# Third feed-forward of an eight-part kernel: weights rounded during the attention before it, maxima and rounding by pieces

## The reference, cut to what matters

```python
x = x + _L2_xattn_ref(_layernorm(x), ctx, ctx, w_q, w_k, w_v, w_o)       # fifth: 16 heads of 64
x = x + _L2_ffn_ref(_layernorm(x), clip_x, clip_down, w_gate, w_up, w_down)  # sixth

def _act_fake_quant(x, clip):            # one scale for the whole tensor
    scale = sigmoid(clip) * max(|x|) / 127
    return clamp(round(x / scale), -128, 127) * scale
def _weight_fake_quant(w):               # one scale for each row
    scale = max(|w|, axis=1) / 127
    return clamp(round(w / scale), -128, 127) * scale
def _L2_ffn_ref(x, clip_x, clip_down, w_gate, w_up, w_down):   # 352 inner units
    xq = _act_fake_quant(x, clip_x)
    h = _act_fake_quant(silu(xq @ Wq(w_gate).T) * (xq @ Wq(w_up).T), clip_down)
    return h @ Wq(w_down).T
```

## Time and profile before

| | us |
|---|---|
| median of three runs | 2153.54 (2153.01 to 2155.19) |
| the profiled execution's own time | 2155.52 |
| its span (what the profile covers) | 2153.7 |
| PE busy | 1917.7 (89%) |
| DVE busy | 1305.2 (61%) |
| ACT busy | 1291.8 (60%) |
| stage `ln2a` starts / `pair_layer` starts | 781.1 / 788.6 |
| `ln2f` starts / `ffn2_stage` starts / `ln3a` starts | 1629.1 / 1636.5 / 1673.7 |

### The profile page before, as it was taken

The page is one execution under the profiler, slowest core; times in us unless marked ns, Lnnn a source line. Parts: engine busy times, 40 slices in busy tenths (PEclk is TensorE's granted clock), DMA queues, the critical chain, the costliest instruction groups (busy, mean ns, idle before and its releaser), DMA issues. The chain is left out here.

```text
span 2153.7 us, 43741 instructions
## 1 busy us (share of the span) xinstructions
PE 1917.7 (89%) x17168; PEld 1360.0 (63%) x17168; DVE 1305.2 (61%) x3216; ACT 1291.8 (60%) x2074; POOL 130.7 (6%) x344
## 2 busy tenths in 40 slices
PE   6999999967768559999999999999994699999997
PEld 4677777734634546777777777777772456666663
DVE  6888888876545335554555545555445776666663
ACT  4999999954248115555555555555553356666664
POOL 4000000000022110000000000000000400000000
PEclk9999999977869669999999999999996789999998
DMA  6211111102070520000000000000000621111110
GB/s 230 57 46 44 44 46 45 38 16 70 8 183 2 153 78 1 1 2 1 1 1 1 2 1 1 2 1 2 1 1 11 199 57 47 42 47 46 46 37 17
DMA packets 55291, 87.71 MB, mean 41 GB/s; under 512 B 9865, under 2 KB 31421, under 8 KB 55089
## 3 DMA queue, kind: packets, MB, share of 16 engines
q1 hardware_dynamic: 54577, 83.87, 13.2%
q0 software_dynamic: 512, 1.05, 0.2%
HBM read 66.93 MB, written 17.96 MB: 39 GB/s over the span
## 5 line engine op out<-in xcount | busy, mean ns | idle before, releaser
L2315 ACT ACTIVATE a_prT<-bank 128x512 f32<-128x512 f32 (+1 forms) x448 | 232.7, 565 | 328.0 <-PE bank L2224 327.8
L1110 DVE CUSTOM_DVE_ANT_0 a_attn_junk<-wide,a_mask 128x801 f32<-128x801 f32 (+1 forms) x256 | 247.4, 991 | 123.2 <-PE wide L942 123.0
L1053 ACT ACTIVATE a_attn_prT<-bank 128x512 f32<-128x512 f32 (+1 forms) x448 | 237.0, 566 | 123.0 <-PE bank L959 110.5
L2340 DVE CUSTOM_DVE_ANT_0 a_sc<-wide,a_zeros 128x1024 f32<-128x1024 f32 (+1 forms) x256 | 243.1, 987 | 91.9 <-PE wide L2210 91.9
L1401 DVE CUSTOM_DVE_ANT_0 a_attn_sc<-wide,a_mask 128x801 f32<-128x801 f32 (+1 forms) x256 | 252.8, 988 | 12.0 <-PE wide L1252 10.2
L1268 PE MATMUL bank<-ident,a_attn_sc 128*128 128x128 f32 x1664 | 244.6, 275 | 15.2 <-ACT a_attn_prT L1360 14.1
L1268 PEld LDWEIGHTS bank<-ident,a_attn_sc 128*128 128x128 f32 x1664 | 198.8, 141 | 62.2 <-issue 42.3
L2224 PE MATMUL bank<-ident,a_sc 128*128 128x128 f32 x1664 | 231.3, 277 | 1.5 <-ACT a_prT L2315 1.5
L2224 PEld LDWEIGHTS bank<-ident,a_sc 128*128 128x128 f32 x1664 | 185.4, 141 | 54.4 <-issue 28.1
L2210 PE MATMUL wide<-a_kT,a_qT 64*128 64x512 f32 (+1 forms) x1024 | 211.0, 529 | 0.0
L2276 PEld LDWEIGHTS bank<-a_prT,a_vt 128*64 128x64 f32 x3328 | 180.3, 137 | 48.4 <-issue 47.0
(11 more groups left out here) (448 smaller groups left out, 2537.5 us busy)
## 6 DMA issues: line engine op xcount, KB each, us to landing
a_ks<-a_k_parts SPq DMA_DIRECT2D x384, 75.0 KB
a_k_parts<-a_proj_kp SPq DMA_DIRECT2D x24, 416.0 KB, 4.3
a_qx<-a_q_stack SPq DMA_DIRECT2D x384, 12.0 KB
moe_w1b<-in_e_w SPq DMA_DIRECT2D x15, 256.0 KB, 2.8
ctxT<-in_ctxT SPq DMA_DIRECT2D x4, 832.0 KB, 10.6
a_ctxn<-in_ctxn SPq DMA_DIRECT2D x4, 832.0 KB
m_q_stack<-m_proj_qp SPq DMA_DIRECT2D x9, 256.0 KB, 8.9
m_ks<-m_k_parts SPq DMA_DIRECT2D x24, 96.0 KB
```

Of the source, the lines that this page charges most:

```text
L1053: act.activation(prT[0:keys, u % PRT, kt:kt + m, :], bank_of(s, f"W{g}")[0:keys, 0:m * S].rearrange("p (t q) -> p t q", q=S), ACT.Exp).the ...
L1110: dve.tensor_tensor_reduce(junk[:, n % 2, 0:w], S_WIDE[n % 2][:, 0:w], mask(qt, at, w), 1.0, LOWEST, ALU.add, ALU.max, mx[:, p % 2, qt, e, ...
L2315: copy = lambda out, src: act.activation(out, src, ACT.Copy)
L2340: dve.tensor_tensor_reduce(sc[:, s % 2, h, at:at + w], S_WIDE[h][:, 0:w], zeros[:, 0:w], 1.0, LOWEST, ALU.add, ALU.max, mx[:, s % 2, h, p: ...
```

## The change

The weights of the sixth block are loaded by `ln2a` instead of `ln2f`, live in SBUF through the attention, and are rounded inside `pair_layer`, on VectorE at the end of steps 44 to 49 (a few instructions in each); ScalarE makes the exponential of the clip factors in step 44. In `ffn2_stage` the spreading of a maximum is one matmul with the column, broadcast along its free axis, as weights and the identity as moving operand, after which every partition takes the maximum of its own copy. `x` is rounded by halves, and the last step (subtracting the constant and writing bfloat16) is ScalarE's. The pieces run through three bank pairs instead of two, all chunks of the first half ahead of the second; VectorE takes each piece's maximum one piece later, and the six maxima are reduced at the end. `h` is rounded by pieces: two VectorE operations and one of ScalarE. The down projection has the tokens' `h` stationary, 24 matmuls of 128 columns, and its output comes untransposed; the scale of `w_down`'s rows is spread once over the partitions (`down_row`), and two VectorE operations for each of four groups of two tiles scale and add.

```diff
--- before.py
+++ after.py
@@ -627,158 +627,154 @@
...
-def ffn2_stage(core, w_gu, w_down, clips):
+def ffn2_stage(core, w, sig):
...
+        g_bank, u_bank, d_bank = core.bank[0:3], core.bank[3:6], core.bank[0:4]
+        tb, tb2 = core.bank[6][:, :].bitcast(BF16), core.bank[7][:, :].bitcast(BF16)
+        row_bank, top_bank = core.bank[5][:, 0:P], (core.bank[4][:, 0:P], core.bank[6][:, 0:P])
+        work = [(c, i) for c in range(2) for i in range(NC)]
...
         @block.tensor
...
+            pe.matmul(row_bank, am[:, 2 * NC:].broadcast_to([P, P]), core.ident[:, :], start=True, stop=True).then_inc(row_made, 1)
+            pe.wait_ge(col_ready, 1)
+            pe.matmul(top_bank[0], col[:, 0:1].broadcast_to([P, P]), core.ident[:, :], start=True, stop=True).then_inc(spread, 1)
+            pe.wait_ge(w_copied, 2)
+            pe.wait_ge(row_in, 1)
+            for n, (c, i) in enumerate(work):
+                if i == 0:
+                    pe.wait_ge(xq_ready, c + 1)
+                if n >= 3:
+                    pe.wait_ge(gu_read, n - 2)
+                rhs = xq[:, c * 512:(c + 1) * 512]
+                pe.matmul(g_bank[n % 3][0:pad(i), :], wgu[:, i, 0:pad(i)], rhs, start=True, stop=True)
+                pe.matmul(u_bank[n % 3][0:pad(i), :], wgu[:, NC + i, 0:pad(i)], rhs, start=True, stop=True).then_inc(gu_ready, 1)
+            pe.wait_ge(col_ready, 2)
+            pe.matmul(top_bank[1], col[:, 1:2].broadcast_to([P, P]), core.ident[:, :], start=True, stop=True).then_inc(spread, 1)
...
+                pe.wait_ge(hq_ready, NC * (c + 1))
...
+                    for i in range(NC):
+                        at = c * 512 + t * P
+                        ins = pe.matmul(d_bank[2 * c + t // 2][:, t % 2 * P:(t % 2 + 1) * P], hq[0:pad(i), i, at:at + P], wd[0:pad(i), i, :],
+                                        start=(i == 0), stop=(i == NC - 1))
+                    if t % 2 == 1:
+                        ins.then_inc(down_ready, 1)
...
         @block.scalar
...
+            act.activation(gs[0:1, 0, 0:1], core.ones[0:1, 0:1], ACT.Silu).then_inc(warm, 1)
...
+            act.wait_ge(row_made, 1)
+            act.activation(down_row[:, :], row_bank, ACT.Copy).then_inc(row_in, 1)
+            act.wait_ge(warm, 1)
+            for c in range(2):
+                cols = slice(c * 512, (c + 1) * 512)
+                act.wait_ge(rounded, c + 1)
+                act.activation(xq[:, cols], xr[:, cols], ACT.Identity, bias=back[:, :]).then_inc(xq_ready, 1)
+            act.wait_ge(scales, 1)
...
+                if n >= 3:
+                    act.wait_ge(gu_read, n - 2)
+                act.activation(gs[0:pad(i), n % 3, :], g_bank[n % 3][0:pad(i), :], ACT.Silu,
...
+            for n, (c, i) in enumerate(work):
+                cols = slice(c * 512, (c + 1) * 512)
+                act.wait_ge(h_rounded, n + 1)
+                act.activation(hq[0:pad(i), i, cols], h[0:pad(i), i, cols], ACT.Identity,
+                               bias=back[0:pad(i), :]).then_inc(hq_ready, 1)
...
         @block.vector
...
+            dve.memset(back[:, :], -ROUND)
+            dve.memset(part[:, :], 0.0)
+
+            def scale_of(r):
+                dve.wait_ge(spread, r + 1)
+                link(dve.tensor_reduce(top[:, r:r + 1], top_bank[r], X, ALU.max))
+                link(dve.tensor_scalar(sx[:, r:r + 1], top[:, r:r + 1], sig[:, r:r + 1], 1.0 / 127.0, ALU.mult, ALU.mult))
...
+            def magnitude(n):
+                c, i = work[n]
+                dve.wait_ge(gu_read, n + 1)
+                return dve.tensor_reduce(part[0:pad(i), n:n + 1], h[0:pad(i), i, c * 512:(c + 1) * 512], X, ALU.max,
+                                         apply_absolute_value=True)
+
+            dve.tensor_reduce(col[:, 0:1], core.xnT[:, :], X, ALU.max, apply_absolute_value=True).then_inc(col_ready, 1)
+            scale_of(0)
+            for c in range(2):
+                cols = slice(c * 512, (c + 1) * 512)
+                link(dve.tensor_scalar(xr[:, cols], core.xnT[:, cols], rx[:, 0:1], ROUND, ALU.mult, ALU.add))
+                dve.tensor_scalar(xr[:, cols], xr[:, cols], ROUND + 127.0, ROUND - 128.0, ALU.min, ALU.max).then_inc(rounded, 1)
+                if c == 0:
+                    dve.tensor_scalar(fs[:, :], am[:, 0:2 * NC], sx[:, 0:1], None, ALU.mult).then_inc(scales, 1)
+            dve.wait_ge(scales, 1)
...
+                dve.scalar_tensor_tensor(h[0:pad(i), i, c * 512:(c + 1) * 512], u_bank[n % 3][0:pad(i), :],
+                                         fs[0:pad(i), NC + i:NC + i + 1], gs[0:pad(i), n % 3, :],
...
+                if n > 0:
+                    magnitude(n - 1)
+            link(magnitude(2 * NC - 1))
+            dve.tensor_reduce(col[:, 1:2], part[:, :], X, ALU.max).then_inc(col_ready, 1)
+            scale_of(1)
+            for n, (c, i) in enumerate(work):
+                piece = h[0:pad(i), i, c * 512:(c + 1) * 512]
+                link(dve.tensor_scalar(piece, piece, rx[0:pad(i), 1:2], ROUND, ALU.mult, ALU.add))
+                dve.tensor_scalar(piece, piece, ROUND + 127.0, ROUND - 128.0, ALU.min, ALU.max).then_inc(h_rounded, 1)
+            dve.wait_ge(row_in, 1)
+            for g in range(4):
+                tiles = core.x[:, 2 * g:2 * g + 2, :]
+                dve.wait_ge(down_ready, g + 1)
+                dve.scalar_tensor_tensor(term[:, g, :, :], d_bank[g][:, 0:2 * D].rearrange("p (t d) -> p t d", d=D),
+                                         sx[:, 1:2], down_row[:, :].unsqueeze(1).broadcast_to([P, 2, D]), ALU.mult,
+                                         ALU.mult).then_inc(scaled, 1)
+                dve.wait_ge(scaled, g + 1)
+                dve.tensor_tensor(tiles, tiles, term[:, g, :, :], ALU.add).then_inc(added, 1)
+            dve.wait_ge(added, 4)
...
@@ -2121,7 +2117,7 @@
...
-def pair_layer(core, name, acc, wq, wk, wv, wo):
+def pair_layer(core, name, acc, wq, wk, wv, wo, quantised):
...
@@ -2153,6 +2149,8 @@
...
+    QUANTISE = STEPS - 20
+    w_chain, sig_ready = core.sem(name + "_w_chain"), core.sem(name + "_sig_ready")
...
@@ -2323,10 +2321,38 @@
...
                         act.activation(sc[:, s % 2, h, 0:SC], sc[:, s % 2, h, 0:SC], ACT.Exp, bias=nmx[:, s % 2, h:h + 1],
...
+                if s == QUANTISE:
+                    act.activation(quantised[-1][:, :], quantised[2], ACT.Exp, scale=-1.0).then_inc(sig_ready, 1)
...
+            link = Link(dve, w_chain)
+            w_gu, w_down, clips, am, inv, wqn, wdq, sig = quantised
+            NC = len(FF2_CHUNKS)
+
+            def quantise(s):
+                if s == QUANTISE:
+                    link(dve.tensor_reduce(am[:, 0:2 * NC], w_gu, X, ALU.max, apply_absolute_value=True))
+                elif s == QUANTISE + 1:
+                    link(dve.tensor_reduce(am[:, 2 * NC:], w_down, X, ALU.max, apply_absolute_value=True))
+                    link(dve.tensor_scalar(am[:, :], am[:, :], 1.0 / 127.0, None, ALU.mult))
+                    link(dve.reciprocal(inv[:, :], am[:, :]))
+                elif s == QUANTISE + 2:
+                    for i in range(2 * NC):
+                        ins = dve.tensor_scalar(w_gu[:, i, :], w_gu[:, i, :], inv[:, i:i + 1], ROUND, ALU.mult, ALU.add)
+                    link(ins)
+                elif s == QUANTISE + 3:
+                    link(dve.tensor_scalar(w_down, w_down, inv[:, 2 * NC:], ROUND, ALU.mult, ALU.add))
+                    link(dve.tensor_scalar(wqn[:, :, :], w_gu, ROUND, 127.0, ALU.subtract, ALU.min))
+                elif s == QUANTISE + 4:
+                    dve.memset(wdq[:, FF2:], 0.0)
+                    link(dve.tensor_scalar(wdq[:, 0:FF2], w_down, ROUND, 127.0, ALU.subtract, ALU.min))
+                elif s == QUANTISE + 5:
+                    dve.wait_ge(sig_ready, 1)
+                    link(dve.tensor_scalar(sig[:, :], sig[:, :], 1.0, None, ALU.add))
+                    link(dve.reciprocal(sig[:, :], sig[:, :]))
+
...
@@ -2367,6 +2393,7 @@
...
                 take(dve, dve.tensor_copy, scaled, s, 9, freed_by_dve)
                 take(dve, dve.tensor_copy, scaled, s, 11, freed_by_dve)
+                quantise(s)
...
@@ -2418,22 +2445,24 @@
...
-            layernorm_stage(core, "ln2a", core.x, core.xn, core.xnT, loads=[
...
+            NC = len(FF2_CHUNKS)
+            am, sig, wqn, wdq = sb("f2_am", [P, 2 * NC + 1]), sb("f2_sig", [P, 2]), sb("f2_wqn", [P, 2 * NC, D], BF16), sb("f2_wdq", [P, NC * P], BF16)
+            with ExitStack() as inner:
+                sbi = lambda n, shape, dt=F32: core.sb(inner, n, shape, dt)
+                wq, wk, wv = (sbi("a2_" + n, [P, HEADS * 64]) for n in ("wq", "wk", "wv"))
+                wo = sbi("a2_wo", [P, HEADS // 2, D])
+                wgu, wdn, clips = sbi("f2_wgu", [P, 2 * NC, D]), sbi("f2_wdn", [P, FF2]), sbi("f2_clips", [P, 2])
+                inv = sbi("f2_inv", [P, 2 * NC + 1])
+                layernorm_stage(core, "ln2a", core.x, core.xn, core.xnT, loads=[
```

(43 more changed lines are left out.)

82 lines of the change are left out of this document (8 added, 74 removed).

## The result

The changed kernel runs in a median of 2146.56 us (2143.43 to 2150.27, eight runs); the kernel before, beside it on the same chip, in 2154.07 (2152.15 to 2155.62, eight runs). The ratio is 0.9963, with a 95% interval of 0.9952 to 0.9974: 8.0 us less (5.6 to 10.3), where 8.9 were forecast.

What follows compares the result with a forecast made beforehand. It took `ffn2_stage` for one serial chain of 36.1 us, nearly all VectorE's. The terms -6.6 - 2.5 - 1.7 + 1.5 + 0.4 = -8.9 us gave 2144.6 from 2153.54, range 2142.5 to 2147.5, with A and C 2141.5 to 2149.

Steps and rivals of the forecast that it cites:

- Up to the first gate matmul: Start of `ffn2_stage`: 6.6 us earlier, from 5.9 for the weights, 0 for the first scale, 0.7 for rounding `x`.
- The first scale: In `ffn2_stage`, from the maximum over `x` to the first rounding: 3.2 us before and after, no gain.
- The rounding of `x`: In `ffn2_stage`, up to the first gate matmul: 2.4 us before, 1.75 by halves, gain 0.7.
- Six pieces: In `ffn2_stage`, first gate matmul to rounding of `h`: 14.0 us to 11.5, gain 2.5, VectorE the bound.
- Rival A: Loads in `ln2a` hidden or pieces overlapping better: -10.8 + 0.4, about 2143 us; chance 12%.
- Rounding of `h` and down projection: End of `ffn2_stage`: 10.5 us to 8.8, gain 1.7.
- Cover in the attention: Six weight portions, each under VectorE's 1.37 us idle stretch, cost 0 in the attention; up to 5.2 us without cover.
- Rival B: Cover in the attention partly gone, portions showing up to 5.2 us: -3.7, 2149.8 us; chance 6%.
- D: Slower rival: portions open gaps in the attention that drop TensorE's clock, 2.15 us each; +9.2, 2162.7 us; chance 2%.
- The loads: Four more loads in `ln2a`, which has no slack: attention starts 1.5 us later, bounds 0.9 to 4.
- rival C: Loads in `ln2a` cost 4 us instead of 1.5, seventh block's clock rises 2 us late: 2148.7 us; chance 8%.
- Clock: TensorE's clock low through both blocks' seams; its rise 0.4 us sooner to 2 us later, +0.4 added.

Runs made afterwards that it cites:

- e6: Changed kernel with two bank pairs and two Silu buffers for the six pieces instead of three; `ln2f` to `ln3a` 34.3 us (+0.8), run 2148.02 us.
- e7: Changed kernel with one maximum over all of `h` behind the six products instead of six among them; `ln2f` to `ln3a` 34.1 us (+0.6), run 2146.44 us.
- e4: Changed kernel with all six portions of weight rounding in one attention step (45); attention 836.81 us, run 2147.22 us.
- e8: Changed kernel with ten more maxima over the gate and up weights in attention step 44; attention 846.19 us, run 2158.81 us.
- e1: Changed kernel with the two clip-factor loads ahead of the large loads of `ln2a`; `ln2a` 10.63 us (after 10.89), run 2146.17 us.
- e2: Changed kernel with the four feed-forward loads still issued in `ln2a` but waited for only in attention step 44; `ln2a` 9.14 us, median 2145.91 us, ratio 0.9947.
- e5: Changed kernel with the four feed-forward loads issued by SP once the attention has begun; `ln2a` 8.24 us, median 2144.68 us, ratio 0.9946 to before.
- e9: Changed kernel with the weights loaded by `ln2f` and rounded in `ffn2_stage` as before; `ln2f` to `ln3a` 38.38 us, run 2150.36 us.
- e10: e5 plus matmuls whose result nobody reads in `ln2a`; attention 834.72 us, median 2140.72 us, ratio 0.9929 to before.

## Why the prediction was right, and where it was off

The forecast of -8.9 us came out at -8.0, with its mechanism: a shorter chain in the sixth block, the portions hidden, SP last in `ln2a`. Of the signs that were to confirm it all came: the first gate matmul at 4.9 us, the stage's end at 25.0, VectorE without a gap among the pieces, SP waiting for the clip factor, TensorE at 80 of 80. But so did one of the three that were to refute it, the attention starting over 3 us later (3.33).

- *Up to the first gate matmul*: 6.6 forecast, 6.7 measured, though its parts were cut wrongly. The weights' 6.0 us are 4.85 from the move and 1.2 from the clearing that went. The first scale gave 0.3, forecast at nothing (from the maximum's start to the first rounding 2.89 instead of 3.23): its matmul waited 0.16 us for TensorE's queue and not 0.4. The rounding of `x` to the first gate matmul gave 0.35 (2.26 to 1.91), half of the 0.7 forecast; my two stretches before overlapped by 0.18 us. The lone float32 matmul, put at 0.75 between 0.58 and 1.0, took 0.69 and 0.80.
- *Six pieces*: 2.5 forecast, 2.6 measured; VectorE is the bound and gapless, as said. The third pair is worth 0.8 of it (e6), the maxima by pieces 0.6 (e7). Rival A, better overlap or hidden loads, did not come.
- *Rounding of `h` and down projection*: 1.7 forecast, 1.8 measured. ScalarE's six take 4.99 us beside VectorE. The stage is 25.0 us long, 25.3 were forecast.
- *Cover in the attention*: right, and larger than the 1.37 us that I argued from. I read the idle stretch ahead of a drain as the whole slack; a late drain only eats into TensorE's lead, and e4 and e8 put the longest portion that it takes between 5.1 and about 6.9 us. Rival B fell with it, and D's trigger was mis-sized too: TensorE waits only from a portion of 6.9 us on, so that my gap of 2.8 us would need 6.9 + 2.8 = 9.7, where I had 2.8 + 1.37 = 4.2. D's price for one gap was 2.15 us for the clock beside the wait; in e8 the clock cost 4.3, since it came back only after 8.6 us of work, not 4.3, and the whole was 9.4.
- *The loads*: the term that was mis-sized, +1.5 forecast, +3.33 measured. With the scatter of the four-load stage taken in it is 2.5 us (8.19 to 10.71). The step "384 + 176 KB more at 372 GB/s are 1.5 us" counts bytes at the full rate only. They did flow so, until 787.6. Behind that came 1.6 us of tail at 68 and 34 GB/s, and then 1.1 us to the attention's start instead of 0.8. e1 shows that the order of the small ones isn't it. So the first half of rival C came in part, inside the bounds. The mechanism (SP last, no slack) was right; e2 and e5 get 1.75 and 2.65 us back by taking the wait away. How much of the tail is each load's own stays open.
- *Clock*: +0.4 guessed, +0.7 in the seventh block of the profiled pair, 0 in the attention; the seventh block took 454.0 to 455.8 us over all profiles, so +0.7 lies inside the scatter. I had read the clock as low through both seams. In fact it was at 1.00 from 1671.0 to 1674.4 in before and from 1648.7 to 1652.1 in after, while TensorE was busy 0.78 and 0.19 us of these 3.4: a rise that came when there was nothing to gain from it.
- *Sum*: -11.0 + 3.33 = -7.7 against -8.9; the 1.8 us on the loads are the miss, less 0.4 for the clock, which I had inside the sum, and 0.2 by which the sixth block is better.

The scatter between runs lies mostly upstream of the change. The self-attention stage takes 115.2 us in after and 120.8 in e4, and the table of windows shows by what, after first:

```profile
680.00:700.00 20.00, 9.70 (x92) 5.54 (x86) 6.00 (x31) 8.66 (x18) 0.41 (x2) 0.91 0.03 7
```

```profile
680.00:700.00 20.00, 14.63 (x100) 7.82 (x98) 3.68 (x12) 8.58 (x19) 0.82 (x4) 0.73 0.00 1
```

Why the clock comes late there in some runs isn't settled. The two scatters go together: the four profiles with the short self-attention stage (115.1 to 115.3 us) are those with the late rise in the attention behind it (840.5), and in e2 to e6 and e9, with 118.4 to 121.1 us, it took about 837. Before and after are both of the first kind, which makes the pair a fair one; that was luck.

## What to carry to other kernels

Work moved from a serial stage into a stage that another engine bounds is free up to the lead of that engine, here between 5.1 and 6.9 us in one step, which is more than the idle stretch that a timeline shows at one instruction; find its edge by piling the work up in one step. Its inputs must move too, and a stage that already ends on a wait for loads pays for more of them at once, with a tail, so issue them where nobody waits. When the rest is tuned, look where the clock rises: matmuls without use ahead of a stage that TensorE bounds took 3.1 us off it (e10 against e5).

## What the runs showed of the hardware

- After a gap of 3.98 us TensorE's clock came back to 2.4 GHz behind 8.6 us of steady work (e8); at the attention's start, with gaps of 0.69 us between the first matmuls, it rose after 5.6 us (e4) and after 15.3 us (after), over instructions that are the same.
- Matmuls without use, in a stage that TensorE otherwise idles in, raised the clock before the attention and saved 2.1 to 5.8 us of it (e10).
- 560 KB and two loads of 0.5 KB behind 2 MB in one wait cost 2.5 us in the mean of the profiles, 1.5 by their bytes at 372 GB/s.
- A pass over 3072 columns in six pieces costs VectorE more (0.67 a piece against 3.35 for a maximum), yet the pieces won, since they fill time beside other engines.
